# Gathered rows transposed in 32x32 blocks by VectorE in the expert stage, and state times C for two state units per GpSimd instruction

## What is computed

```python
# 1: selective state space model on the context, gated by layernorm(x)
delta, B, C, u = ...                       # from the context, per batch
state = state * exp(delta * A) + delta * u * B     # 16 states per channel, over 1024 steps
y     = sum over the 16 states of state * C        # + D * u, * silu(z)
x     = x + tanh(g_xattn) * y
# 2: mixture of experts on xn = layernorm(x), 4096 tokens
topk_idx, topk_w = gate(xn)                # 4 of 32 experts for a token
buf[e, c]  = xn[token]                     # at most 256 rows for each expert
h  = silu(buf @ w1) * (buf @ w3);  ob = h @ w2     # per expert: 1024 -> 512 -> 1024
x  = x + tanh(g_ffn) * (sum of topk_w * ob + shared expert(xn))
```

## Time and profile before

| | |
|---|---|
| time, median of 3 runs | 4099.43 us (4098.16 to 4102.16) |
| profiled execution, its span | 4099.1 us |
| scan stage, first to last scan | 492.2 to 1717.7 us |
| PE busy | 3803.9 us (93%) |
| DVE busy | 3017.5 us (74%) |
| ACT busy | 2141.8 us (52%) |
| POOL busy | 1727.5 us (42%) |
| POOL, state times C (L1116) | x512, 1205.3 us, mean 2409 ns |
| DVE, scans (L1099) | x512, 1135.0 us, mean 2272 ns |

### The profile page before, as it was taken

How to read it: one execution, slowest core, us unless ns; L and a number is a source line. 1 busy time by engine, 2 the same in 40 slices (tenths; PEclk the granted TensorE clock), 3 DMA queues, 4 the chain that set the end, 5 groups by cost and what they waited for, 6 DMA issues and landing times. The chain is left out here.

```text
span 4099.1 us, 60052 instructions
## 1 busy us (share of the span) xinstructions
PE 3803.9 (93%) x21088; PEld 3147.7 (77%) x21088; DVE 3017.5 (74%) x3711; ACT 2141.8 (52%) x2768; POOL 1727.5 (42%) x977
## 2 busy tenths in 40 slices
PE   8898588888888888799999989999999999999999
PEld 3444488788888788678888878888888888788887
DVE  7898799999999999877777755555555555455555
ACT  3688699889889989722222244444444444200000
POOL 0243299999999999823333310000000000122222
PEclk9999599999999999999999999999999999999999
DMA  6687843643643643355555656677777766677543
GB/s 236 241 294 259 299 141 114 180 140 109 185 140 110 184 140 117 132 198 179 182 187 187 222 197 236 236 240 241 237 244 239 234 235 235 221 281 267 199 164 118
DMA packets 328298, 819.60 MB, mean 200 GB/s; under 512 B 65920, under 2 KB 109696, under 8 KB 318784
## 3 DMA queue, kind: packets, MB, share of 16 engines
q1 hardware_dynamic: 296240, 750.13, 54.4%
q0 software_dynamic: 31744, 67.23, 5.5%
q10 hardware_dynamic: 144, 0.00, 0.0%
HBM read 603.38 MB, written 245.27 MB: 207 GB/s over the span
## 5 line engine op out<-in xcount | busy, mean ns | idle before, releaser
L1116 POOL TENSOR_TENSOR h<-h,c 128x1024 f32<-128x1024 f32 x512 | 1205.3, 2409 | 27.6 <-DVE h L1099 23.9
L1099 DVE TENSOR_TENSOR_SCAN h<-da,dbu 128x1024 f32<-128x1024 f32 x512 | 1135.0, 2272 | 50.1 <-ACT dbu L1061 28.7
L1148 PE MATMUL psy<-ident,h 128*128 128x128 f32 x4096 | 562.4, 281 | 81.6 <-POOL h L1116 60.0
L1069 ACT ACTIVATE da<-dl,ad 128x1024 f32<-128x1024 f32 x512 | 583.7, 1140 | 100.5 <-DVE h L1099 88.5
L1061 ACT ACTIVATE dbu<-psb 128x512 f32<-128x512 f32 x1020 | 547.9, 589 | 34.1 <-PE psb L1138 32.0
L1148 PEld LDWEIGHTS psy<-ident,h 128*128 128x128 f32 x4096 | 445.1, 143 | 129.6 <-POOL h L1116 90.9
L1947 POOL DMA_INDIRECT xg<-scratch_xn,ids x62 | 61.3, 989 | 1010.2 <-PE psT L1965 997.8
L2105 DVE TENSOR_TENSOR wsp<-arena,wsp 128x2048 fp32r<-128x2048 f32 x146 | 329.9, 2286 | 77.3 <-ACT wsp L2059 77.3
L1605 ACT ACTIVATE hT_s<-psH_s 128x512 fp32r<-128x512 f32 x64 | 38.2, 598 | 625.1 <-PE psH_s L1533 625.1
L1138 PE MATMUL psb<-m,du_taps 128*128 128x128 f32 x2048 | 294.0, 290 | 43.9 <-ACT dbu L1061 35.7
L1138 PEld LDWEIGHTS psb<-m,du_taps 128*128 128x128 f32 x2048 | 258.6, 193 | 79.7 <-ACT dbu L1061 73.0
(11 more groups left out here) (232 smaller groups left out, 8253.8 us busy)
## 6 DMA issues: line engine op xcount, KB each, us to landing
arena<-in_w SPq DMA_DIRECT2D x192, 1024.0 KB, 6.1
du_taps<-scratch_duT SPq DMA_DIRECT2D x496, 128.0 KB, 2.9
c<-scratch_c SPq DMA_DIRECT2D x64, 512.0 KB, 12.5
scratch_xT<-xT_s SPq DMA_DIRECT2D x32, 1024.0 KB, 4.8
scratch_ob<-ob SPq DMA_DIRECT2D x64, 512.0 KB, 2.9
xT_place<-scratch_xT SPq DMA_DIRECT2D x32, 1024.0 KB, 6.3
scratch_duT<-duT SPq DMA_DIRECT2D x52, 512.0 KB, 4.2
xz<-in_x SPq DMA_DIRECT2D x32, 512.0 KB, 5.4
```

Source lines behind the costliest of these rows:

```text
L1069: act.activation(da[k % 2][:, :], dl[:, i % 2, :], ACT.Exp, scale=ad[:, i % 2, n:n + 1]).then_inc(s_da, 1)
L1099: dve.tensor_tensor_scan(h[:, k % HR, :], da[k % 2][:, :], dbu[:, (k // GN) % 2, k % GN, :], 0.0, ALU.mult, ALU.add).then_inc(s_scan, 1)
L1116: pool.tensor_tensor(h[:, k % HR, :], h[:, k % HR, :], c[:, n, :], ALU.mult).then_inc(s_hc, 1)
L1148: mm = pe.matmul(psy[:, t, :], h[:, k % HR, t * P:(t + 1) * P], ident[:], is_transpose=True, start=(n == 0 and t % 4 == 0), stop=(n == NST ...
```

## The change

Scan stage: POOL multiplies two consecutive units by two rows of C in one instruction of 128x2048, behind the scan of the second. The ring `h` has six units in place of four, BEHIND is 8 in place of 6, and the gate stands behind n = 2 in place of n = 1. To make room, `c` holds 14 rows: states 14 and 15 use the places of 6 and 7, and these four rows are loaded anew in every tile (`stream_c`).

Expert stage: the x rounds are gone from PE. POOL gathers quarters of rows (eight indirect DMAs per expert, 128 pieces of 1 KB each, in place of two of 4 KB pieces), so placed that one DVE transpose of 32x32 blocks of a 128x1024 tile gives the columns that are needed. For that the routing pass stores `scratch_xn` in another order of columns, four DMAs per tile with 128-byte pieces. The ids are loaded as 32-partition pieces of eight 4-byte words (four DMAs per expert), and POOL adds the number of the quarter to them. ACT and DVE make head and rest of the transposed rows over 1024 columns at once, from SBUF.

```diff
 # selective_scan
-        HR = 4
-        AHEAD, BEHIND = 3, 6
-        GATED, SKIPPED = 1, 6
+        HR = 6
+        AHEAD, BEHIND = 3, 8
+        GATED, SKIPPED = 2, 6
+        PAIR = 2
+        SHARED = (6, 14)
...
-        c = sb("c", [P, NST, L])
+        c = sb("c", [P, NST - PAIR, L])
...
+            def stream_c(i, first):
+                before = i * NST + first - NH
+                after(sp, s_hc, before // PAIR + 1 if before >= 0 else 0)
+                for n in range(first, first + PAIR):
+                    sp.dma_start(c[:, c_place(n)], dr["c"][i // ET, n].partition_broadcast(P)).then_inc(s_cl[n], 16)
...
                 if i:
+                    stream_c(i, SHARED[0])
                     store(i - 1)
...
                         load_du(i + 1, r)
+                    if r == 2:
+                        stream_c(i, SHARED[1])
...
-                pool.wait_ge(s_scan, k + 1)
-                pool.tensor_tensor(h[:, k % HR, :], h[:, k % HR, :], c[:, n, :], ALU.mult).then_inc(s_hc, 1)
+                if n % PAIR == PAIR - 1:
+                    pool.wait_ge(s_scan, k + 1)
+                    first = (k - PAIR + 1) % HR
+                    states = h[:, first:first + PAIR, :].rearrange("p a l -> p (a l)")
+                    rows = c[:, c_place(n) - PAIR + 1:c_place(n) + 1, :].rearrange("p a l -> p (a l)")
+                    pool.tensor_tensor(states, states, rows, ALU.mult).then_inc(s_hc, 1)
...
-                pe.wait_ge(s_hc, k + 1)
+                pe.wait_ge(s_hc, k // PAIR + 1)
 # shared_pass, route: SP, then POOL at the end
-                        sp.dma_start(xnd[t], xn[:, par, :]).then_inc(s_xnst[par], 16)
+                        for q in range(NQ):
+                            sp.dma_start(xnd[t][:, q * HQ:(q + 1) * HQ].rearrange("p (j c) -> p j c", c=QB),
+                                         xn[:, par, :].rearrange("p (j q c) -> p q j c", q=NQ, c=QB)[:, q]).then_inc(s_xnst[par], 16)
...
-                for r in range(2 * TPE):
-                    sp.dma_start(ids[:, r:r + 1], tab[r]).then_inc(early["ids"][r], 16)
+                for e in range(2):
+                    for q in range(NQ):
+                        sp.dma_start(ids_of(ids, e)[q * QB:(q + 1) * QB, :], id_rows(dr, e), allow_slow_non_contiguous=True).then_inc(early["ids"][e], 16)
...
+                pool.wait_ge(early["ids"][0], 16 * NQ)
+                pool.tensor_tensor(ids_of(ids, 0), ids_of(ids, 0), ids[:, QUARTER:QUARTER + SETQ], ALU.add).then_inc(s_quarter, 1)
+                pool.wait_ge(s_quarter, 1)
                 for t in range(TPE):
-                    pool.wait_ge(early["ids"][t], 16)
                     pool.sem_inc(s_carry, 1)
-                    pool.indirect_dma_start(xg[:, t, :], None, dr["xn"],
...
+                    for g in range(NQ):
+                        gather_quarters(pool, dr, ids, xg, 0, t, g).then_inc(early["gat"][t], 16)
 # experts: POOL
+                pool.tensor_tensor(ids_of(ids, x), ids_of(ids, x), ids[:, QUARTER:QUARTER + SETQ], ALU.add).then_inc(s_quarter, 1)
+                pool.wait_ge(s_quarter, e)
                 for t in range(TPE):
+                    pool.wait_ge(s_xlo, TPE * (e - 1) + t + 1)
                     pool.sem_inc(s_carry, 1)
+                    for g in range(NQ):
+                        gather_quarters(pool, dr, ids, xg, x, t, g).then_inc(s_gat[t], 16)
 # experts: PE (h rounds become h_transpose, each with its own psT)
-                round_of("h", 0, 0)
-                round_of("x", 0, 0)
+                h_transpose(e, 0)
                 gate_up(e, x, 1, 1, range(KH // 2, KH))
...
                 down(e, x, 1, 0)
-                round_of("x", 1, 0)
-                round_of("x", 1, 1)
                 down(e, x, 1, 1)
 # experts: DVE
+            def x_blocks(e, t):
+                gathered(dve, e, t)
+                dve.transpose(xg[:, t, :], xg[:, t, :]).then_inc(s_xt, 1)
+            def x_rest(e, t):
+                dve.wait_ge(s_xhi, TPE * e + t + 1)
+                dve.tensor_tensor(columns(t, 1), blocks(t), f32(columns(t, 0)), ALU.subtract).then_inc(s_xlo, 1)
...
                 matrix_rest(e + 1, x + 1, 1, 0)
+                if not last:
+                    x_blocks(e + 1, 0)
                 multiply(e, 0)
                 matrix_rest(e + 1, x + 1, 1, 1)
-                split(e, rest, "h", 0, 0)
+                h_rest(e, 0)
+                if not last:
+                    x_blocks(e + 1, 1)
                 multiply(e, 1)
-                split(e, rest, "x", 0, 0)
-                split(e, rest, "h", 1, 0)
+                if not last:
+                    x_rest(e + 1, 0)
+                h_rest(e, 1)
...
                 out_half(e, 0)
-                split(e, rest, "x", 0, 1)
-                split(e, rest, "x", 1, 0)
+                if not last:
+                    x_rest(e + 1, 1)
                 out_half(e, 1)
-                split(e, rest, "x", 1, 1)
```

More of the change, by code:

```diff
@@ L34 @@
 LINE = 64
+QB = 32
+NQ = P // QB
+HQ = H // NQ
+SETQ = TPE * NQ
+QUARTER = 2 * SETQ
 ALU = mybir.AluOpType
@@ L938, in selective_scan, with c_place @@
         f32 = lambda ap: ap.bitcast(F32)
+        def c_place(n):
+            return n if n < SHARED[1] else n - SHARED[1] + SHARED[0]
+        streamed = [n + j for n in SHARED for j in range(PAIR)]
         def units(body):
@@ L970, in load_c @@
             def load_c(b, n):
-                after(sp, s_hc, (b * ET - 1) * NST + n + 1 if b else 0)
-                sp.dma_start(c[:, n], dr["c"][b, n].partition_broadcast(P)).then_inc(s_cl[n], 16)
+                if n not in streamed:
+                    after(sp, s_hc, ((b * ET - 1) * NST + n) // PAIR + 1 if b else 0)
+                    sp.dma_start(c[:, n], dr["c"][b, n].partition_broadcast(P)).then_inc(s_cl[n], 16)
+            def stream_c(i, first):
[3 more added lines that the diff above has]
+                    sp.dma_start(c[:, c_place(n)], dr["c"][i // ET, n].partition_broadcast(P)).then_inc(s_cl[n], 16)
             def load_u(i):
@@ L1371, in _ @@
             for s in (*((*s_xnst, *s_x1st, *s_xtst) if route else ()), *s_acst):
-                sp.wait_ge(s, 16 * TT // 2 - (16 if route and s is s_acst[1] else 0))
+                sp.wait_ge(s, 16 * TT // 2 * (NQ if route and s in s_xnst else 1) - (16 if route and s is s_acst[1] else 0))
         if route:
@@ L1847, in experts @@
         f32 = lambda ap: ap.bitcast(F32)
-        ROUNDS = [("h", 0, 0), ("x", 0, 0), ("h", 1, 0), ("x", 0, 1), ("x", 1, 0), ("x", 1, 1)]
-        H_DONE = (1, 3)
-        X_DONE = (4, 6)
         halves = (slice(0, WN // 2), slice(WN // 2, WN))
-        NR = len(ROUNDS)
-        HEAD = 2 * TPE
-        def rounds(e):
-            last = isinstance(e, int) and e == NE - 1
-            kept = [r for r in ROUNDS if r[0] == "h" or not last]
-            return [(kind, t, hb, HEAD + e * NR + n, n % 2) for n, (kind, t, hb) in enumerate(kept)]
         DONE = 4
@@ L1954, in _, with h_transpose @@
         def _(pe):
-            def transpose_round(kind, t, hb, n, bank, e):
-                if kind == "h":
-                    pe.wait_ge(s_h, TPE * e + t + 1)
-                else:
-                    gathered(pe, e, t)
-                after(pe, s_tlo, n - 1)
-                src = sg[:, t, :] if kind == "h" else xg[:, t, hb * HB:(hb + 1) * HB]
-                for k in range(4):
-                    mm = pe.transpose(psT[bank][:, k, :], src[:, k * P:(k + 1) * P], ident[:])
-                mm.then_inc(s_tr, 1)
+            def h_transpose(e, t):
+                pe.wait_ge(s_h, TPE * e + t + 1)
+                after(pe, s_hlo, TPE * (e - 1) + t + 1 if not (isinstance(e, int) and e == 0) else 0)
+                for k in range(KF):
+                    mm = pe.transpose(psT[t][:, k, :], sg[:, t, k * P:(k + 1) * P], ident[:])
+                mm.then_inc(s_htr, 1)
             def product(dst, lhs, rhs, done, ks, ready=None):
@@ L2000, in expert @@
             def expert(e, j, x):
-                first, last = isinstance(e, int) and e == 0, isinstance(e, int) and e == NE - 1
-                turn = {(kind, t, hb): (n, bank) for kind, t, hb, n, bank in rounds(e)}
-                def round_of(kind, t, hb):
-                    if (kind, t, hb) in turn:
-                        transpose_round(kind, t, hb, *turn[kind, t, hb], e if kind == "h" else e + 1)
                 for t in range(TPE):
-                    pe.wait_ge(s_tlo, 2 * t + 2 if first else HEAD + (e - 1) * NR + X_DONE[t])
+                    pe.wait_ge(s_xlo, TPE * e + t + 1)
                     gate_up(e, x, 0, t)
@@ L2022, in expert, with blocks @@
                 down(e, x, 1, 0)
-                round_of("x", 1, 0)
-                round_of("x", 1, 1)
                 down(e, x, 1, 1)
-            for n in range(HEAD):
-                transpose_round("x", n // 2, n % 2, n, n % 2, 0)
             turns(pe, NE // XT, four(expert), last=True)
-        def split(e, step, *which):
```

(34 more changed lines are left out.)

107 lines of the change are left out of this document (57 added, 50 removed).

## The result

| | before | after |
|---|---|---|
| time, median | 4098.8 us (4096.4 to 4102.2) | 4271.4 us (4261.1 to 4276.4) |
| ratio, 95% interval | | 1.0419 (1.0404 to 1.0433) |
| span of the profiled execution | 4099.1 us | 4270.1 us |

The change makes the kernel 4.2% slower; I had forecast 4093 us, no change. The stages show where the time goes. The two spans differ by 171.0 us. The limits of the stretches are starts of instructions in the timelines: first scan, last gate, last product of the routing pass (`psO_s`), first gate product of the experts (`psG`), first of the last stage (`psG_s`).

A forecast was written before the change was run, and what follows sets the result against it. POOL was taken to bound the scan stage, with DVE close behind, and PE the expert stage. From 4099.1 us, +32 (scan stage), -49 (experts) and +11 (between the passes) gave 4093 us, range 4050 to 4135.

The forecast's parts named there:

- What bounds the kernel: Scan stage: POOL is the limit, DVE next with about 1 us per tile of room; expert stage: PE, always busy.
- the rival by which the scan stage gains: Scan stage: PE's addition not held by ACT's copy, DVE runs at 37.0 per tile, -25, total 4036 us; chance 0.15.
- The pair: Scan stage, POOL: one instruction for two units takes 4.51 us as distance, 4.61 as duration, so POOL stops being the limit.
- no cheaper than two singles: Rival, scan stage: POOL's pair costs as much as two singles; +30, total 4123 us; chance 0.12.
- The gate's chain: Scan stage: gate waits through ACT's copy and PE's addition; DVE stands 1.87 us, not 0.75; 1.0 us more per tile.
- Streaming of C: Scan stage: four rows of C per tile, 2 MB, issued 15 us or more before POOL needs them, costed at nothing.
- small pieces: Rival: small pieces fill DMA engines; late routing loads +50, 4143 us, or late expert weights +31, 4124; chance 0.10.
- Or over 39.5: Sign against the prediction, scan stage: gates over 39.5 us apart, where 38.8 was forecast.
- Changes of batch: Scan stage: where batches change, the streamed rows of C and SP's wait cost some microseconds each.
- Experts, -49: Expert stage: taking the x transposes from PE saves 1.58 us for each of 31 experts, -49 us.
- Between the passes, +11: Routing to expert 0: later gathers, block transposes and PE at its lower clock add 11 us (7 to 14).
- Routing pass: Routing pass: 4096 pieces of 128 bytes per tile in place of 128 of 4 KB cost nothing, from 0 to +50.

The follow-up runs named there:

- du_gate3: Kernel of after_du_first with GATED = 3 instead of 2, so DVE gates a tile behind its third following scan; 4090.5 us.
- after_du_first: Changed kernel with the second pair of streamed rows of C issued behind the four loads of `du`, not in front of the last; 4156.9 us.
- unstreamed: Changed kernel without the four rows of C streamed per tile; units 14 and 15 multiply by the rows of 6 and 7; 4147.7 us.
- after_ids: Changed kernel with the tensor of row numbers `ids` at its old size, 1024 bytes per partition instead of 96; 4237.3 us.

## Why the prediction was wrong, point by point

- **What bounds the kernel.** Right: POOL at 98%, DVE next with room of 1 us per tile. du_gate3 reached 36.7 us, close to the 37.0 that I gave for DVE alone in the rival by which the scan stage gains. That rival needed one scan more in front of the gate.
- **The pair**, 4.61 us: right, 4.60 on the page of the profile after. The rival "no cheaper than two singles" is out. The Trainium skill (GPSIMD Engine Reference, Elementwise — side-by-side cycle accounting) has 4497 ns for an addition of 2048 elements. The trace has 4596 for this multiplication, 2% more.
- **The gate's chain.** The mechanism and the size of its wait were right (1.87 forecast, 1.86 measured once `du` was in time). The term of 1.0 us per tile was too small: I let the next group's start "give back 0.13". There DVE waits 0.4 us where PE's clock is low for 3.4 us, and 1.1 to 1.7 where it is low for 6.8. I had the waits of DVE in the sum but not those that they cause behind it, at ACT (3.2 us) and PE (2.8), and above all not PE's clock. Without any streaming the 25 tiles lost 1.66 us each, 41 us, not the 25 that a term of 1.0 gives.
- **Streaming of C, "I cost them at nothing".** This is the step that failed. It was worth 114 us for the order alone, by after_du_first, and 124 in all, by unstreamed (which also loads two rows of C less per batch). In the scan stage the +184.5 us are 125.2 for the streaming (1417.4 - 1292.2), where I had 0, and 59.3 for the rest (1292.2 - 1232.9), where I had 32. Of the 59.3, 41 lie in the quiet tiles, 13 around changes of batch and 5 before the first gate. The prediction looked at when POOL needs the rows, 15 us after their issue. It never asked what stands behind them on SP's queue, and how much time that has: `du` portion 3, with four units. The mean DMA share of 0.47 in the earlier trace rows hid it, for what counts is the 5 us in which it is 1.04. No rival of mine had this; the "small pieces" one looked at the wrong transfers. "Or over 39.5" in the list of what would prove me wrong did catch it.
- **Changes of batch**, "some microseconds each": 33 us for three in after, 13 of them still without streaming.
- **Experts, -49.** The mechanism was right: with the old places the stage takes 1085.5 us in after_ids, -52.2, 1.76 per expert instead of the 1.58 forecast. Block transposes took 1.24 us (1.2 forecast), the gathers of expert 0 are 1.31 apart (1.35), and PE waits only once, 1.1 us, in the first expert. The term missing was the place of the tensors: 20 us here and 12 in the last stage. The smaller `ids` is named ahead of the prediction as all that changes in the last stage; the prediction has no line for it.
- **Between the passes, +11**: +5.8. The first gather came 0.4 us later instead of 2.3 after the last product (3.5 against 3.1), and the barrier stands 4.9 behind the eighth gather's start where it stood 6.9 behind the second's.
- **Routing pass, nothing:** right, +2.4 from last gate to last product. 4096 pieces of 128 bytes in each of 32 tiles changed the stage by at most those 2.4 us; the trace has no wait for them. One reading was wrong: "half of each tile DMA does nothing". The earlier trace rows show 5 us without transfers, and a tile takes some 21 (669.9 / 32). The Trainium skill (DMA: Bandwidth & Descriptors, Specifications) says that below 512 bytes a read-modify-write is made. No run here shows whether one was.

## What to carry to other kernels

For each DMA that an edit adds, name the transfer behind it on its queue, the time from when that one may start to when its data are wanted, and the DMA share in exactly those microseconds; a mean share over a stage says nothing about it. When a wait lands on the engine that feeds the others, follow it once round the loop (here DVE, ACT, PE and PE's clock) before giving it a price; here the clock alone made 1 us of difference between tiles with the same waits. After any change of a buffer's size compare the distances of matmuls in untouched stages, not their durations.

## What the runs showed of the hardware

- Where operands lie in SBUF can cost TensorE 3%: with `ids` at 96 bytes instead of 1024 or 512 the matmuls 128x128 by 128x512 with `xT_place` came 233 ns apart instead of 227, at full clock, in stages where PE is 99% busy. That made 32 us in all, from the size of one tensor of row numbers. Why is open.
- TensorE ran at half clock (0.50) for 3.4 or 6.8 us behind waits of 2.8 us, and for 6.8 us around a wait of 4.4. The longer drop made a tile 1 us longer. In the quiet tiles of du_gate3 before the last, where no wait of PE is longer than 1.03, it kept 1.00.
- Behind two broadcast rows of C, 1 MB, the last of four loads of 128 KB landed 7 us or more after its issue (1323.05 less 1313.23 + 2.60), where the median of such loads is 3.0; with the two rows behind it, PE waited for it in no quiet tile.
- One POOL instruction over 2048 columns costs 4.60 us and two over 1024 cost 4.82; a pair is 4.5% cheaper, but its first unit is ready later by 2.2 us of the longer instruction and by the 2.2 of the second scan that it waits for.
